# Waits carried by the instructions that need them, and the output projection in the order Wo, transposes, V

## The reference, cut to what matters

```python
xn = layernorm(x)                                   # 8 x 1024 x 256
a  = sliding_window_attn(xn, Wq, Wk, Wv, Wo)        # 16 heads of 16, blocks of 64 queries over 192 keys
h  = layer_norm(a + xn) * g1 + b1
f  = gelu(h @ W1 + c1) @ W2 + c2                    # 256 -> 1024 -> 256
attn_branch = layer_norm(f + h) * g2 + b2
moe_branch  = xn + expert_w[argmax(xn @ gate_w.T)] @ xn   # 8 experts, 256 x 256 each
out = x + attn_branch + moe_branch
```

## Time and profile before

| what | value |
|---|---|
| median of the runs | 1336.77 us (3 runs, 1333.58 to 1338.08) |
| the profiled execution's own time | 1332.42 us |
| its span, first to last instruction | 1330.7 us |
| PE busy | 1142.8 us (86%) |
| DVE busy | 897.5 us (67%) |
| ACT busy | 728.9 us (55%) |
| POOL busy | 676.1 us (51%) |
| mean granted TensorE clock | 0.972 of full |

### The profile page before, as it was taken

One profiled execution on the slowest core, in us unless ns is written; L12 is line 12 of the kernel. 1 busy time (PEld: TensorE's weight loads), 2 busy tenths in 40 slices (PEclk: granted clock), 3 DMA queues, 4 the chain that ended last, 5 costly groups with the idle time before them and its releaser, 6 DMA issues.

```text
span 1330.7 us, 32163 instructions
## 1 busy us (share of the span) xinstructions
PE 1142.8 (86%) x11726; PEld 675.3 (51%) x11726; DVE 897.5 (67%) x2105; ACT 728.9 (55%) x1498; POOL 676.1 (51%) x856
## 2 busy tenths in 40 slices
PE   0636898899979998899989999899988999799887
PEld 0323446564537536474546636374455645375446
DVE  8564657676677757676677756677576766776455
ACT  1322776448563675538564585627764485636771
POOL 5410574527752575507743476516745277524851
PEclk9957999999999999999999999999999999999989
DMA  8594288234942369234973259333872249422010
GB/s 276 127 235 145 90 176 179 84 102 137 230 129 90 135 133 212 68 121 133 203 144 111 86 136 239 88 113 117 182 173 92 94 135 230 129 72 90 14 20 33
DMA packets 126230, 176.43 MB, mean 133 GB/s; under 512 B 11104, under 2 KB 95968, under 8 KB 122976
## 3 DMA queue, kind: packets, MB, share of 16 engines
q1 hardware_dynamic: 103168, 132.43, 34.6%
q0 software_dynamic: 22912, 41.95, 17.2%
HBM read 82.85 MB, written 85.07 MB: 126 GB/s over the span
## 4 chain that ended last, share of the span: by engine, by line
PE 60%; DVE 12%; ACT 11%; issue 8%; POOL 5%; DMA 2%; another core or an unknown queue 2%; SPq 0%; POOLq 0%; DVEq 0%; ACTq 0%
PE bank L1387 8%; PE bank L1273 7%; PE bank L1172 5%; PE bank L1173 5%; PE bank L1175 5%; PE bank L1265 4%; PE bank L1481 4%; DVE m_sb L763 3%; PE bank L1478 3%; PE bank L1477 3%; PE bank L1204 2%; ACT bank L1109 2%; ACT pool L1054 2%; ACT pool L995 2%; PE bank L1240 2%
## 5 line engine op out<-in xcount | busy, mean ns | idle before, releaser
L1054 ACT ACTIVATE pool<-bank 128x512 f32<-128x512 f32 x512 | 279.1, 599 | 91.4 <-PE bank L1273 88.8
L763 DVE TENSOR_REDUCE m_sb<-bank 128x2 f32<-128x384 f32 x512 | 259.7, 552 | 89.5 <-PE bank L1281 70.3
L500 POOL TENSOR_SCALAR_AFFINE_SELECT pool<-pool 128x512 f32<-128x512 f32 x256 | 191.4, 749 | 128.2 <-ACT pool L1054 87.2
L438 POOL TENSOR_TENSOR rs<-ve,neghalf 128x1 f32<-128x1 f32 x64 | 36.8, 575 | 305.0 <-DVE ve L840 252.8
L1387 PE MATMUL bank<-pool,v_a 128*32 128x256 f32 (+2 forms) x2560 | 155.7, 335 | 12.9 <-POOL pool L505 9.5
L1265 PE MATMUL bank<-k_s,q_s 48*64 48x192 f16 x2048 | 95.3, 260 | 82.8 <-DVE m_sb L763 71.5
L1040 ACT ACTIVATE xn<-bank 128x256 f32<-128x256 f32 x120 | 46.1, 384 | 191.8 <-PE bank L1175 174.6
L1273 PE MATMUL bank<-q_s,k_s 128*128 128x256 f16 (+1 forms) x1024 | 138.2, 274 | 11.1 <-ACT pool L1054 6.3
L855 DVE TENSOR_TENSOR pool<-bank,pool 128x512 f16<-128x512 f32 x128 | 88.2, 689 | 65.9 <-ACT pool L1068 56.5
L505 POOL TENSOR_SCALAR_AFFINE_SELECT pool<-pool 128x512 f32<-128x512 f32 x200 | 130.8, 654 | 0.0
L1109 ACT ACTIVATE bank<-bank,c1c 128x512 f32<-128x512 f32 x128 | 84.7, 662 | 77.6 <-PE bank L1175 39.6
(11 more groups left out here) (174 smaller groups left out, 2443.1 us busy)
## 6 DMA issues: line engine op xcount, KB each, us to landing
pair_dram<-pool SPq DMA_DIRECT2D x96, 256.0 KB
xn<-xs_dram SPq DMA_DIRECT2D x40, 384.0 KB, 3.8
ys_dram<-xn SPq DMA_DIRECT2D x120, 128.0 KB, 1.8
q_s<-pair_dram SPq DMA_DIRECT2D x32, 384.0 KB
k_s<-pair_dram SPq DMA_DIRECT2D x32, 384.0 KB
x_sb<-in_L_attn_x SPq DMA_DIRECT2D x8, 1024.0 KB, 6.5
res_dram<-in_L_attn_x SPq DMA_DIRECT2D x8, 1024.0 KB, 7.1
res_dram<-xn POOLq DMA_DIRECT2D x8, 1024.0 KB, 7.8
```

Source lines behind the costliest of these rows:

```text
L500: nc.gpsimd.affine_select(out=p, in_=p, compare_op=ALU.is_ge, fill=0.0, base=0, pattern=[[0, 4], [1, 2 * W]], channel_multiplier=-1).then_ ...
L763: nc.vector.tensor_reduce(m_sb[:, 4 * g + par:4 * g + 4:2, t], max_bank(j, par)[:, 0:2 * WIN].rearrange("p (h c) -> p h c", h=2), AX.X, AL ...
L1054: nc.scalar.activation(prob[:, (k + 2) % 3, par::2, :], score_bank(k, par)[:, :].rearrange("p (h q) -> p h q", h=2), ACT.Exp, scale=EXP_SC ...
```

## The change

Three things are done at once.

1. All increments of `passed` go, and the semaphore with them, so that nearly every wait is carried by the instruction behind it. The two waits ahead of `scores` become one (VectorE's count only rises, so the higher value covers the lower), and so do the two ahead of `scores_t_pair`. The semaphore instructions that are left number 316 on PE, 85 on DVE, 139 on ACT, 33 on POOL and 33 on SP.
2. Waits that another wait already covers go: in `exps` that for `pv`, in `normalize` that for `t2_ps`, in ScalarE's copy `aT` that for `wo_ps`, in `b_stage` those of T1 for `att` and of T2 for `aT_ev`, in `w1_unit` and `w2_part` those for earlier values of the same count.
3. In `b_stage` on TensorE a step's products stand in another order: Wo of tile s-4, T2 of tile s-2, T1 of tile s, V of tile s+1. VectorE's and ScalarE's own order stays.

The core of the diff; the same `passed` line goes in some thirty more places:

```diff
@@ scores_wait
-            def scores_wait(b, j, par, first=False):
-
-                u = 2 * j + (1 if par == 0 else 0)
-                if j == 0 and par == 1:
+            def scores_wait(b, j, first=False):
+                if j == 0:
                     pe.wait_ge(v_ev.sem, v_ev.at(b, T))
-                    pe.sem_inc(passed, 1)
                     pe.wait_ge(stack[0].sem, stack[0].at(b, 64))
-                    pe.sem_inc(passed, 1)
...
-                    pe.wait_ge(mx.sem, mx.at(b, u - 3))
-                    pe.sem_inc(passed, 1)
-                elif not first or u >= 2:
-                    pe.wait_ge(mx.sem, mx.at(b, u - 1))
-                    pe.sem_inc(passed, 1)
+                    pe.wait_ge(mx.sem, mx.at(b, 2 * j - 2))
+                elif j or not first:
+                    pe.wait_ge(mx.sem, mx.at(b, 2 * j))
@@ scores_t_wait
-                elif u >= 2:
-                    pe.wait_ge(ex_done.sem, ex_done.at(b, u - 1))
-                    pe.sem_inc(passed, 1)
+                if k:
+                    pe.wait_ge(ex_done.sem, ex_done.at(b, 2 * k + par - 1))
@@ band on GpSimd
                 pool.wait_ge(ex_done.sem, ex_done.at(b, 2 * k + 2))
-                pool.sem_inc(passed, 1)
@@ maxima on VectorE
                     dve.wait_ge(S_ps.sem, S_ps.at(b, 2 * j + n + 1))
-                    dve.sem_inc(passed, 1)
@@ normalize on VectorE
                 dve.wait_ge(rc.sem, rc.at(b, t + 1))
-                if t >= 2:
-                    dve.wait_ge(t2_ps.sem, t2_ps.at(b, t - 1))
@@ exps on ScalarE
-                if k >= 3:
-                    act.wait_ge(pv.sem, pv.at(b, k - 2))
@@ ScalarE's copy aT
                     act.wait_ge(t2_ps.sem, t2_ps.at(b, t + 1))
-                    if t >= 2:
-                        act.wait_ge(wo_ps.sem, wo_ps.at(b, t - 1))
@@ b_stage on TensorE
                 for s in range(T + 4):
+                    if s >= 4:
+                        t = s - 4
+                        pe.wait_ge(aT_ev.sem, aT_ev.at(b, t + 1))
+                        if t >= 2:
+                            pe.wait_ge(r1.sem, r1.at(b, t - 1))
+                        for c in range(DC):
+                            mm = nc.tensor.matmul(OB[t % 2][:, 0:D], aT[:, t % 2, c, :], wo[:, c, :], start=(c == 0), stop=(c == DC - 1))
+                        mm.then_inc(wo_ps.sem, 1)
+                    if 2 <= s < T + 2:
+                        t = s - 2
+                        pe.wait_ge(att.sem, att.at(b, t + 1))
+                        for c in range(DC):
+                            mm = nc.tensor.transpose(TB[t % 2][:, c * P:c * P + P], attn[:, t % 2, c * P:c * P + P], ident[:, :])
+                        mm.then_inc(t2_ps.sem, 1)
                     if s < T:
...
-                        if t >= 2:
-                            pe.wait_ge(att.sem, att.at(b, t - 1))
                         for g in range(G):
                             mm = nc.tensor.transpose(MB[t % 2][:, g * P:g * P + P], oT[:, g, t * P:t * P + P], ident[:, :])
                         mm.then_inc(t1_ps.sem, 1)
                         if t + 1 < T and not last:
                             v_tile(b + 1, t + 1)
-                    if 2 <= s < T + 2:
-                        t = s - 2
-                        pe.wait_ge(att.sem, att.at(b, t + 1))
-                        if t >= 2:
-                            pe.wait_ge(aT_ev.sem, aT_ev.at(b, t - 1))
...
-                    if s >= 4:
-                        t = s - 4
...
@@ w1_unit
-                else:
-                    pe.wait_ge(nT_l.sem, nT_l.at(b, DC * hf + DC))
```

More of the change, by code:

```diff
@@ L245, in build @@
         f2 = count("f2", T, credit=TH + 1)
-        passed = ctx.enter_context(nc.semaphore("passed"))
         block = ctx.enter_context(nc.Block())
@@ L307, in stack_loads @@
                     sp.wait_ge(ST_ps.sem, ST_ps.at(b - 1, 4 * T * (c + 1)))
-                    sp.sem_inc(passed, 1)
                 sp.wait_ge(pair_st[i % 2].sem, pair_st[i % 2].at(b, 48 * (i // 2 + 1)))
@@ L1036, in y_out @@
                 act.wait_ge(y_ps.sem, y_ps.at(b, i + 1))
-                act.sem_inc(passed, 1)
                 if i >= 2:
@@ L1281, in mask_mm @@
                 return nc.tensor.matmul(dst, ident16[r, :], band, start=False, stop=True, skip_group_check=True)
-            def scores_wait(b, j, par, first=False):
-                u = 2 * j + (1 if par == 0 else 0)
-                if j == 0 and par == 1:
+            def scores_wait(b, j, first=False):
+                if j == 0:
                     pe.wait_ge(v_ev.sem, v_ev.at(b, T))
-                    pe.sem_inc(passed, 1)
                     pe.wait_ge(stack[0].sem, stack[0].at(b, 64))
-                    pe.sem_inc(passed, 1)
-                if j == 2 * T and par == 1:
+                if j == 2 * T:
                     pe.wait_ge(stack[1].sem, stack[1].at(b, 64))
-                    pe.sem_inc(passed, 1)
                 if j == LEAD:
                     pe.wait_ge(mT_ev.sem, mT_ev.at(b, 2))
-                    pe.sem_inc(passed, 1)
                 elif j > LEAD:
@@ L1299, in scores_wait @@
                         pe.wait_ge(mT_ev.sem, mT_ev.at(b, 3))
-                        pe.sem_inc(passed, 1)
-                    pe.wait_ge(mx.sem, mx.at(b, u - 3))
-                    pe.sem_inc(passed, 1)
-                elif not first or u >= 2:
-                    pe.wait_ge(mx.sem, mx.at(b, u - 1))
-                    pe.sem_inc(passed, 1)
+                    pe.wait_ge(mx.sem, mx.at(b, 2 * j - 2))
+                elif j or not first:
+                    pe.wait_ge(mx.sem, mx.at(b, 2 * j))
             def scores(b, j, first=False):
-                for par in (1, 0):
-                    scores_wait(b, j, par, first)
+                scores_wait(b, j, first)
                 t = j % T
@@ L1329, in scores_t_wait, with scores_t_pair_wait @@
                 g, t = divmod(k, T)
-                u = 2 * k + par
                 if k == 0 and par == 0:
                     pe.wait_ge(y_ev.sem, y_ev.at(b, NT))
-                    pe.sem_inc(passed, 1)
                 if t == 0 and par == 0:
                     pe.wait_ge(mrow[g % 2].sem, mrow[g % 2].at(b, 32 * (g // 2 + 1)))
-                    pe.sem_inc(passed, 1)
+                if k:
+                    pe.wait_ge(ex_done.sem, ex_done.at(b, 2 * k + par - 1))
+            def scores_t_pair_wait(b, k):
+                g, t = divmod(k, T)
+                if t == 0:
+                    pe.wait_ge(mrow[g % 2].sem, mrow[g % 2].at(b, 32 * (g // 2 + 1)))
                 if k == SCORES_FREE:
                     pe.wait_ge(mT_ev.sem, mT_ev.at(b, G))
-                    pe.sem_inc(passed, 1)
-                elif k > SCORES_FREE:
-                    pe.wait_ge(ex_done.sem, ex_done.at(b, u - 3))
-                    pe.sem_inc(passed, 1)
-                elif u >= 2:
-                    pe.wait_ge(ex_done.sem, ex_done.at(b, u - 1))
-                    pe.sem_inc(passed, 1)
+                else:
+                    pe.wait_ge(ex_done.sem, ex_done.at(b, 2 * k - 2))
             def scores_t(b, k, par):
@@ L1354, in scores_t_pair @@
             def scores_t_pair(b, k):
-                for par in range(2):
-                    scores_t_wait(b, k, par)
+                scores_t_pair_wait(b, k)
                 for i in range(2):
@@ L1411, in b_stage @@
                             v_tile(b + 1, t + 1)
-                    if 2 <= s < T + 2:
-                        t = s - 2
-                        pe.wait_ge(att.sem, att.at(b, t + 1))
-                        if t >= 2:
-                            pe.wait_ge(aT_ev.sem, aT_ev.at(b, t - 1))
-                        for c in range(DC):
-                            mm = nc.tensor.transpose(TB[t % 2][:, c * P:c * P + P], attn[:, t % 2, c * P:c * P + P], ident[:, :])
-                        mm.then_inc(t2_ps.sem, 1)
-                    if s >= 4:
-                        t = s - 4
-                        pe.wait_ge(aT_ev.sem, aT_ev.at(b, t + 1))
-                        if t >= 2:
-                            pe.wait_ge(r1.sem, r1.at(b, t - 1))
-                        for c in range(DC):
-                            mm = nc.tensor.matmul(OB[t % 2][:, 0:D], aT[:, t % 2, c, :], wo[:, c, :], start=(c == 0), stop=(c == DC - 1))
-                        mm.then_inc(wo_ps.sem, 1)
             def n1_transposes(b, u, last=False):
@@ L1465, in w2_part @@
                 if part == 0:
-                    pe.wait_ge(g_lo.sem, g_lo.at(b, FC * (hf + 1)))
                     if t >= 2:
                         pe.wait_ge(r2.sem, r2.at(b, t - 1))
-                    elif t == 1:
-                        pe.wait_ge(g_lo.sem, g_lo.at(b, 2 * FC))
-                    elif not last:
+                    else:
+                        pe.wait_ge(g_lo.sem, g_lo.at(b, FC * (t + 1)))
+                    if t == 0 and not last:
                         pe.wait_ge(route.sem, route.at(b + 1, 6))
```

9 lines of the change are left out of this document (removed).

## The result

The changed kernel took 1313.51 us, median of 4 runs (1311.39 to 1319.02), beside 1335.17 for 4 runs of the kernel before (1332.04 to 1338.08). The ratio is 0.9845, 95% interval 0.9804 to 0.9885: 15 to 26 us less on the 1336.8 of the front. The forecast was 1329, 8 us less, with a range down to 1318. Two later comparisons of the same two kernels gave smaller gains; they stand further down.

What follows compares the result with a forecast made beforehand. The prediction took TensorE's own rate to set most of the time, the rest being loops where engines wait for each other. Terms -12.5 + 5.0 - 0.5 = -8.0 us took 1336.8 to 1328.8, rounded to 1329; range 1318 to 1338.

Steps and rivals of the forecast that it cites:

- D: Rival, slower: T1 late in the b_stage step delays both halves' statistics, 11 us, waits give only 6: 1342; chance 0.08.
- E: Rival: engines still pay the same latency when they carry the wait, leaving the order's loss: 1342; chance 0.02.
- Term 1: Late waits on the chain, all engines: 0.05 to 0.10 us saved each, 1.44 us a sequence, -12.5 us (-15.3 to -8).
- The split over engines: Of 21 late-wait pieces on one sequence's chain, 11 lie on PE, 4 on DVE, 4 on ACT, 2 on POOL.
- Term 2: End of b_stage: the new order brings the transposes 0.63 us later in each of eight sequences, +5.0 us (0 to +6.5).
- Covered waits: Waits in exps, normalize, copy aT and on PE already covered by others: removing them priced at nothing.
- Term 3: Some ten chain pieces of issue without a semaphore, perhaps instruction fetches: -0.5 us with +-3, bound ten times 0.95 us.
- rival B: Waits gain more, all 21 pieces and late waits beside the chain count, order costs little: 1320; chance 0.20.
- C: Rival: waits hide behind other paths, -6 us, and the order costs its 5: 1335.5, no visible change; chance 0.20.

Runs made afterwards that it cites:

- inc_first: Kernel before with each wait and increment swapped in 39 of 40 places, so the wait rides on the real instruction and the increment stands ahead: ratio 0.9896, -13.9 us.
- pe_waits: Kernel before with only TensorE's waits of the change, old order in b_stage: ratio 0.9947, -7.1 us.
- others_waits: Kernel before with only the waits of VectorE, ScalarE, GpSimd and SyncE changed, old order: ratio 0.9892, -14.4 us.
- no_incs: Kernel before with only the idle semaphore's increments deleted, covered and doubled waits kept: ratio 0.9844 to the kernel before, -20.9 us.
- bare_pe: Changed kernel with the old b_stage order and 1634 idle increments added on TensorE ahead of its waits: ratio 0.9931 to the kernel before.
- waits_only: Changed kernel with TensorE's old b_stage order and the two waits that order needs: ratio 0.9840 to the kernel before, -21.4 us.
- waits_third: Repeat of the changed kernel with the old b_stage order and the waits it needs: 1309.58 us, ratio 0.9817 to the kernel before.
- after_third: The changed kernel run once more, in a later comparison: 1315.64 us, ratio 0.9868 to the kernel before.

## Why the prediction was wrong, step by step

- **Which way and why: right.** The waits gain, the order gives part of it back. Nothing speaks for D or E.
- **Term 1, late waits, -12.5 us: right in size.** inc_first, which has this effect without fewer instructions, gave -13.9 (-11.4 to -16.4). The 0.10 us of a late wait is in the trace after. The split over engines isn't tested: pe_waits and others_waits (7.1 for 7.0, 14.4 for 5.5) hold the effect of the number too.
- **Term 2, the order, +5.0: right.** Between +4.5 and +6.1 in three comparisons, +1.6 with a wide interval in the fourth, and the places of `b_stage` within 0.1 us of those forecast. That the sum comes out so well is helped by two small errors: the order alone is 0.62 us a sequence for the 0.72 forecast, and the 0.08 taken off it for a wait may be counted in term 1 already.
- **Covered waits, nothing: not refuted.** 0.9844 with them, 0.9840, 0.9839 and 0.9817 without. The doubled wait of the scores costs its 0.10 us where it is late, as above.
- **Term 3, "Fetches ... I take term 3 as -0.5 us with +-3": the step that failed.** It measured about -7 (inc_first to no_incs, 3 to 11). I had seen the pieces of issue without a semaphore, named them, bounded their gain at ten times 0.95 us, and then taken next to nothing, because I saw no way to tell which of them would go. Fewer instructions don't only move the stops; they make them fewer: in the changed kernel TensorE has none. The ten were not all of one kind either. Four, 4.1 us in all (152.47, 466.89, 771.57 and 1226.11 in the chain before), stand at the place in 256 found above. That of 539.29 isn't one: the gelu behind it starts at 540.34, when the W1 unit that it needs has ended at 540.30. So TensorE's stops account for some 4 of the 7 us, and the rest has no place in the trace.
- **The rest.** -13.9, -7.0 and +5.7 give 1321.6, near rival B's 1320. The first comparison, 0.9845, is 1316.1 by the ratio (1313.5 as measured), the other two of the changed kernel, 0.9882 and 0.9868, are 1321.0 and 1319.2, and their intervals overlap with that of the first. So some 5 us of the miss may lie in how wide a comparison of four runs each is, and not in the kernel; by the other two the time would stand just inside the range, with twice the forecast gain.
- **The range.** It took +-3 for the fetches and reached to B's centre. With the bound of 9.5 us that the text itself had for them it would have begun at B's 1320 less 9.5, some 1311. (C's own terms make 1335.8, not 1335.5, which changes nothing.)

## What to carry to other kernels

An increment or a second wait that stands alone behind a late semaphore costs about 0.1 us at each place where an engine is waited for, and more than in proportion once it makes punctual waits late. Instructions that do nothing cost time even off the path: in a fully unrolled kernel of 32,000 instructions some 1900 of them were about 7 us (3 to 11). So count them, look for stops inside a group of equal products, and see whether these stand at one place of every 256 instructions. When two edits come together, try each alone: here the order took back a quarter of what the waits gave.

## What the runs showed of the hardware

- TensorE can stop for 0.5 to 3.8 us in the middle of a group with nothing to wait for, and all such stops here stand at one place of every 256 instructions of its own list. The Trainium skill (Runtime: NRT & Kernel Launch, Instruction fetch mechanics) calls the cost of crossing a fetched block "mostly hidden"; the rows of bare_pe (10.1 us of idle time in five breaks) and of the kernel before (3.2 us in three) don't agree. No row names the stops as fetches; their places and the queues' packets do.
- The same program takes 1303 us in some comparisons and 1334 in others, and some 25 of the 31 us between the traces of waits_only and waits_third lie ahead of the scores in one stretch, the W1 units. There ScalarE's gelu waits some 4 us in each of seven sequences; in after_again, of the faster kind, that wait is absent. From the waits of the changed kernel, in us in total, times, longest:

```profile
ACT bank L1076 <- remote: 30.0, 7, 4.4
```

The expectation of after_third put it down to stores. The chain of the changed kernel says otherwise:

```profile
534.99 0.60 ACT pool L1037
535.59 4.20 another core or an unknown queue
539.79 0.02 issue
539.81 0.67 ACT bank L1076
```

The wait for the stores stands ahead of L1037, which runs before the idle time, and the gelu behind it asks for TensorE's count of W1 units alone. That count rises twice within 0.08 us, at 539.79 and 539.86, while a unit takes TensorE 1.3 us. So TensorE's own results come late here, at the same unit in each of the seven sequences. Why, and why only in some comparisons, was not tried.
